# Later value products, quarter pieces as filler and more banks in the last attention stage of a one-core transformer kernel

## The reference, cut to what matters

```python
def _L1_xattn_ref(k, q, v):                      # k = v = context (16, 64, 512), q = layernorm(x)
    scores = jnp.einsum('bcn,bcm->bnm', k, q) / jnp.sqrt(jnp.float32(input_dim))
    attn = jax.nn.softmax(scores, axis=-1)       # over m: a 512 x 512 matrix for each batch entry
    return jnp.einsum('bnm,bcm->bcn', attn, v)
def _L1_ffn_ref(x, W_org, lora_down, lora_up, lora_keys, Wq):   # x = layernorm(x) of the new x
    base = jnp.einsum('bsi,oi->bso', x, W_org)
    q = jnp.einsum('bi,ki->bk', x.mean(axis=1), Wq)
    coeffs = jax.nn.softmax(jnp.einsum('bk,ek->be', q, lora_keys) / math.sqrt(K), axis=-1)
    h = jnp.einsum('bsi,eir->bser', x, lora_down)
    return base + jnp.einsum('be,bser,ero->bso', coeffs, h, lora_up)
x = x + _L1_xattn_ref(ctx, _layernorm(x), ctx)
x = x + _L1_ffn_ref(_layernorm(x), ...)
```

## Time and profile before

| | us |
|---|---|
| device time, median of 3 runs | 1195.75 (1193.85 to 1198.1) |
| device time of the profiled execution | 1194.14 |
| its span | 1192.3 |
| TensorE busy | 1124.5 (94%) |
| VectorE busy | 753.9 (63%) |
| ScalarE, GpSimd busy | 542.5 (46%), 416.8 (35%) |
| mean granted TensorE clock | 0.988 |

### The profile page before, as it was taken

How to read it: one execution, slowest core, us unless ns; L and a number is a source line. 1 busy time by engine, 2 the same in 40 slices (tenths; PEclk the granted TensorE clock), 3 DMA queues, 4 the chain that set the end, 5 groups by cost and what they waited for, 6 DMA issues and landing times. The chain is left out here.

```text
span 1192.3 us, 19230 instructions
## 1 busy us (share of the span) xinstructions
PE 1124.5 (94%) x6643; PEld 961.4 (81%) x6643; DVE 753.9 (63%) x1572; ACT 542.5 (46%) x1437; POOL 416.8 (35%) x421
## 2 busy tenths in 40 slices
PE   4899999999999999999999988799999999798998
PEld 3799999899899899999989887567777777676776
DVE  6555555555555555555555777889864666687863
ACT  4444454554544544544444545333323445454531
POOL 4443323323332232332332433144422324554531
PEclk9999999999999999999999999989999999898999
DMA  6211011111101101101100110122202245133300
GB/s 211 76 36 32 23 37 32 29 32 31 35 25 32 37 23 32 36 24 31 37 23 4 40 30 1 27 72 80 76 26 54 62 107 124 44 77 74 89 2 36
DMA packets 48716, 56.49 MB, mean 47 GB/s; under 512 B 10822, under 2 KB 29270, under 8 KB 48620
## 3 DMA queue, kind: packets, MB, share of 16 engines
q1 hardware_dynamic: 48620, 55.26, 17.2%
HBM read 40.56 MB, written 2.10 MB: 36 GB/s over the span
## 5 line engine op out<-in xcount | busy, mean ns | idle before, releaser
L378 PE MATMUL bank<-wqkv,kvT 128*128 128x256 f32 x1536 | 199.8, 286 | 8.7 <-DVE vv L566 8.7
L423 PE MATMUL bank<-wo,aoT 128*128 128x512 f32 x768 | 192.0, 399 | 5.7 <-DVE acc L562 5.7
L378 PEld LDWEIGHTS bank<-wqkv,kvT 128*128 128x128 f32 x1536 | 188.0, 192 | 10.4 <-DVE vv L566 10.4
L366 PE MATMUL bank<-wqkv,kvT 128*128 128x512 f32 x768 | 188.5, 395 | 1.7 <-DVE qn L576 1.7
L423 PEld LDWEIGHTS bank<-wo,aoT 128*128 128x128 f32 x768 | 139.5, 188 | 33.4 <-DVE aoT L557 6.3
L366 PEld LDWEIGHTS bank<-wqkv,kvT 128*128 128x128 f32 x768 | 141.5, 190 | 28.8 <-issue 1.8
L662 POOL TENSOR_TENSOR rms<-msq,half_neg 128x4 f32<-128x4 f32 x64 | 64.5, 1008 | 220.4 <-DVE msq L573 220.2
L874 PE MATMUL bank<-x2T,wgu 128*128 128x512 f32 (+1 forms) x336 | 91.5, 416 | 0.0
L549 ACT ACTIVATE prob<-bank,nmax 128x128 f32<-128x128 f32 x256 | 90.3, 372 | 2.1 <-DVE nmax L586 2.1
L1905 POOL TENSOR_TENSOR pr<-pr,rc 128x512 f32<-128x512 f32 x64 | 66.7, 1045 | 69.6 <-DVE rc L1774 69.5
L665 POOL TENSOR_TENSOR rms<-msq,half_neg 128x2 f32<-128x2 f32 x64 | 44.6, 697 | 132.0 <-DVE msq L582 132.0
(11 more groups left out here) (176 smaller groups left out, 2207.0 us busy)
## 6 DMA issues: line engine op xcount, KB each, us to landing
wqkv_raw<-in_L_xattn_Wq_dram SPq DMA_DIRECT2D x32, 256.0 KB, 2.5
wo_raw<-in_L_xattn_Wo_dram SPq DMA_DIRECT2D x32, 256.0 KB, 2.6
qS<-qhl SPq DMA_DIRECT2D x32, 256.0 KB, 3.7
kS<-chl SPq DMA_DIRECT2D x32, 128.0 KB, 3.0
packed<-_L_ffn_gate_qweight_dram SPq DMA_DIRECT2D x40, 64.0 KB, 2.4
packed<-in_L_ffn_up_qweight_dram SPq DMA_DIRECT2D x40, 64.0 KB, 2.3
packed<-_L_ffn_down_qweight_dram SPq DMA_DIRECT2D x10, 256.0 KB
acc<-in_x_dram SPq DMA_DIRECT2D x8, 256.0 KB, 5.7
```

The source lines that it names most:

```text
L366: mm = pe.matmul(b_q[:, :], kvT[:, l, kt, p, 1:3, :], wqkv[:, par, r, kt, 0:QW], start=(kt == 0 and n == 0), stop=(kt == KT - 1 and n == 2))
L378: mm = pe.matmul(b_kv[:, b * 256:(b + 1) * 256], kvT[:, l, kt, p, 2 * b:2 * b + 2, :], wqkv[:, par, r, kt, QW:QKV], start=(kt == 0 and n = ...
L423: mm = pe.matmul(b_o[:, :], aoT[:, l, h, :, :], wo[:, par, r, h, :], start=(h == 0 and n == 0), stop=(h == G - 1 and n == 2))
```

## The change

Up to tile 23 the lags stay at 5 and 6 steps. From tile 24 (FAR) on, the weights come 6 steps after the scores and the values 8 steps after, and the values are the last thing in TensorE's step. `pmT` and the row buffer `pr` get a third place each from FAR on. The scores have two banks (2 and 5) from tile 26, the weights two (3 and 7) from tile 22. `base` and `delta` are cut into quarters of 3 matmuls and placed by a new table; the first three quarters of a `base` already stand in steps 24 to 28. The small products get banks of their own and an own place (`pe_small`). The loop has 72 steps where it had 71.

```diff
-        LT, LV, LY = 5, 6, 10
-        SLOTS = TILES + LY - 3
+        SLOTS = TILES + 8
+        FAR = 6 * KT
+        TWO_S, TWO_T = 26, 22
...
+        def weights_slot(t):
+            return t + 5 if t < FAR else t + 6
+        def values_slot(t):
+            return t + 6 if t < FAR else t + 8
+        def sum_slot(n):
+            return values_slot(KT * n + KT - 1) + (n < FAR // KT)
...
-            return PT_ * (q - 1) + 6
+            return PT_ * q - 2 if PT_ * q <= FAR else PT_ * q + 5
...
-            return PT_ * p + 16
+            return sum_slot(2 * p + 1) + (2 if sum_slot(2 * p + 1) < WIDE else 3)
...
-            last = k >= WIDE or k == FFN_END
-            if last and 0 <= k - LV < TILES:
-                pe_values(pe, k - LV)
+            t = VALUES_AT.get(k)
+            last = t is not None and k == FFN_END
+            if last:
+                pe_values(pe, t)
             if k == FFN_END:
+                pe_late(pe, k, 0)
                 pe_extra(pe, k)
             pe_piece(pe, k, 0)
             if k != FFN_END:
                 pe_extra(pe, k)
+            pe_small(pe, k)
             pe_piece(pe, k, 1)
-            if not last and 0 <= k - LV < TILES:
-                pe_values(pe, k - LV)
+            if t is not None and not last:
+                pe_values(pe, t)
...
+        LATE = {
+            (24, 0): (("base", 0, 0),),
+            (25, 0): (("base", 0, 1),),
+            (28, 0): (("base", 0, 2),),
+            (30, 0): (("base", 0, 3),),
+            (32, 1): (("rank", 0, 0), ("rank", 0, 1),),
...
+            (47, 0): (("delta", 1, 3),),
+            (49, 0): (("base", 2, 0), ("base", 2, 1),),
+            (50, 1): (("rank", 4, 0), ("rank", 4, 1),),
...
         def pe_base(pe, p, r):
...
-                if p < HP and p % 2 == 0:
-                    pe.wait_ge(s_hv4, KT * (p // 2 + 1))
-                elif p < HP:
+                if p == 0:
+                    pe.wait_ge(s_hval, 2 * FT)
+                elif p <= HP:
                     pe.wait_ge(s_y4, p)
...
-            if r == 0:
-                pe.wait_ge(s_upl, KT)
-                pe.wait_ge(s_hl4, KT * (p // 2 + 1))
+            pe.wait_ge(s_hl4, KT * (p // 2) + r + 1)
...
-            if 25 <= k <= 28:
-                t = k - 25
+            if 30 <= k <= 33:
+                t = k - 30
                 act.wait_ge(s_ld_u, 16)
                 act.wait_ge(s_d, 2 * FT)
                 act.activation(up[:, HI, t, :], uraw[:, t, :], ACT.Copy).then_inc(s_uph, 1)
...
         def pe_l1f(pe):
+            for p in (4, 5):
+                for r in range(KT):
+                    pe_delta(pe, p, r)
+            pe_base(pe, 6, 0)
+            pe_base(pe, 6, 1)
             extra_evicted(pe, x4_slot(PAIRS - 2))
             x4_transposes(pe, PAIRS - 1)
```

More of the change, by code:

```diff
@@ L1243, in extra_evicted @@
                 pe.wait_ge(s_smc, 2)
-            elif kind == "query":
-                pe.wait_ge(s_smc, 3 + 2 * n)
-            elif kind == "scores":
-                pe.wait_ge(s_cv, 5 * n + 1)
-            else:
-                pe.wait_ge(s_smc, 4 + 2 * n)
+        SUMMED = {sum_slot(n): n for n in range(B)}
+        WEIGHTS_AT = {weights_slot(t): t for t in range(TILES)}
+        VALUES_AT = {values_slot(t): t for t in range(TILES)}
         def pair_at(k, first):
@@ L1449, in pe_values @@
                 pe.wait_ge(s_hval, FT + ALONE)
-            elif m == 0 and n == 6:
-                pe.wait_ge(s_y2, PAIRS)
+            elif n == FAR // KT - 1 and m == 0:
+                pe.wait_ge(s_y2, HP + 3)
             elif m == 0:
-                pe.wait_ge(s_ve, 2 * n if n < 6 else 2 * (n - 1))
+                pe.wait_ge(s_ve, 2 * n)
             pe.wait_ge(s_p1l, t + 1)
             for part in (HI, LO):
-                mm = pe.matmul(v_bank(n)[:, :], vS[:, q % 2, m, 2 * b:2 * b + 2, :], pmT[:, t % 2, part, :],
+                mm = pe.matmul(v_bank(n)[:, :], vS[:, q % 2, m, 2 * b:2 * b + 2, :], pmT[:, pm_of(t), part, :],
@@ L1468, in block_kernel @@
-        LATE.update({(61, 0): ("rank", 8), (62, 0): ("rank", 9), (63, 0): ("rank", 10), (64, 0): ("rank", 11),
-                     (64, 1): ("base", 4, 0), (65, 0): ("base", 4, 1), (65, 1): ("base", 5, 0),
-                     (66, 0): ("base", 5, 1), (66, 1): ("delta", 4, 0), (67, 0): ("delta", 4, 1),
-                     (69, 0): ("delta", 5, 0), (69, 1): ("delta", 5, 1), (70, 0): ("base", 6, 0)})
-        RANK_DONE = {k + 1: (piece[1],) for (k, h), piece in LATE.items() if piece[0] == "rank"}
@@ L1475, in pe_piece @@
+        RANK_DONE = {}
+        for (k, h), pieces in LATE.items():
+            for kind, n, r in pieces:
+                if kind == "rank" and r == 1:
+                    RANK_DONE.setdefault(k + 1, []).append(n)
+        DELTA_DONE = {k + 1: n for (k, h), pieces in LATE.items() for kind, n, r in pieces
+                      if kind == "delta" and r == KT - 1}
         def pe_piece(pe, k, h):
@@ new lines, in pe_base, with pe_rank @@
+            for k, (lp, rp) in enumerate(PASSES):
+                pe.matmul(m_o[p][:, :], x4_tile(lp, p)[:, r, :], woT[:, rp, r, :],
+                          start=(r == 0 and k == 0), stop=False)
+        def pe_rank(pe, n, r):
+            c, j = divmod(n, KT)
+            if r == 0:
+                pe.wait_ge(s_dnl, KT)
+                pe.wait_ge(s_x4l, 2 * (c + 1))
+                if j == 0 and c < 3:
+                    pe.wait_ge(s_smc, 4 + 2 * c)
+                elif n == 3 * KT + 1:
+                    pe.wait_ge(s_p1l, TILES)
+                elif n == 3 * KT + 2:
+                    pe.wait_ge(s_x4l, PAIRS)
+                    pe.wait_ge(s_mean, PAIRS)
+                elif n == 3 * KT + 3:
+                    pe.wait_ge(s_hv4, n - 2)
+                else:
+                    pe.wait_ge(s_hv4, n)
+            cols = slice(c % 2 * CW, (c % 2 + 1) * CW)
+            for kt in (2 * r, 2 * r + 1):
@@ L1595, in pe_extra @@
                 pe_key_scores(pe, n)
-            else:
+            elif kind == "weights":
                 pe_coefficients(pe, n)
@@ L1882, in dve_l1f @@
             x4_apply(dve, PAIRS - 1)
+            add_out(dve, 4)
             add_out(dve, 5)
@@ L1917, in pool_slot @@
                 pool_queries(pool, q + 1)
-            p = pair_at(k, PT_ + LY - KT)
-            if p is not None:
-                ln_power(pool, X4, p)
+            if k in SUMMED and SUMMED[k] % 2 == 1:
+                ln_power(pool, X4, SUMMED[k] // 2)
             if 20 <= k <= 23:
```

256 lines of the change are left out of this document (147 added, 109 removed).

## The result

| | median, us | runs |
|---|---|---|
| before | 1196.87 | 1193.85 to 1198.1, 4 runs |
| changed | 1184.45 | 1183.17 to 1185.31, 4 runs |

The ratio is 0.9899, with a 95% interval of 0.9876 to 0.9922: 9 to 15 us less. The forecast was 1177 (1168 to 1187).

A forecast was written before the change was run, and what follows sets the result against it. TensorE was taken to lose 36.1 us from step 24 on, largely waiting on a nearly equally loaded VectorE. Losses of 15.7 plus 2 for clock left 17.7, so 18.4 less; forecast median 1177 us, range 1168 to 1187.

The forecast's parts named there:

- queue rival: Waits at the head of VectorE's step tie TensorE through most of steps 31 to 63; 1182 to 1188 us, chance 0.27.
- hand walk: New lists walked step by step with measured durations; median 1177 us, own range 1170 to 1183, chance 0.62.
- The bare work: TensorE's work from step 24: 5.2, 10.4, 79.8 and 44.1 us by stretch, 139.5 against 139.4 before.
- Steps 25 to 30: VectorE has 14 to 15 us, TensorE 10.4; step 31 comes 14.9 us after step 25, lost 4.5.
- The clock: 2 us added for one or two clock drops, since a stall of 2 us still stands.
- Steps 31 to 63: TensorE has 79.8 us of work beside 80 of VectorE; 8.0 us lost.
- The waits at out(1) and at `rank`: Steps 31 to 51: 2.3 us for `base` of pair 2 behind out(1), and 0.4 to 1.1 at single `rank` products.
- Steps 64 on: Loss of 2.5 us: 0.8 for out(3), 0.6 for a `rank`, 1.1 at the last `x4` and the coefficients.
- I cost this at nothing: Steps 30 to 36: GpSimd gets about 17 us of work, covered by two steps; up to 2 us without cover.
- Values behind the pieces: Values two steps behind the weights, last in the step: the 2.10 us wait for the low part gets two steps of play.
- The clock rival: Low clock comes in steps 25 to 31 and stays or returns; at 60 us low the time is 1205, chance 0.05.
- The signs: Step 31 about 15 us after step 25, low-part waits nearly gone, VectorE about 90% busy, at most two low-clock stretches.

The follow-up runs named there:

- b_spread: Kernel before with the last three halves of `base` and `delta` of each couple moved by 1, 2 and 3 steps; 1193.12 us, ratio 0.9979.
- a_keys_first: Changed kernel with pair 4's normalised rows made early and the two stacked-key DMAs issued before the wait for the queries; 1183.94 us, ratio 0.9896.
- a_end: Changed kernel with pair 6's statistics in step 64, out(3) ahead of them, and pair 6's `x4` behind `rank` 8; 1181.36 us, ratio 0.9872.
- a_queries_early: Changed kernel with pair 4's normalised rows made ahead of entry 4's sum and copied ahead of the exponential; 1184.33 us, ratio 0.9894.

## Why the prediction was right, and where it was off

The side, the place and the kind of the gain were right, the size was too large: 18.8 us of gain were forecast against the median of its time, 12.4 came. The range held because it took in a part of the queue rival: the range that the hand walk gave itself, 1170 to 1183, doesn't hold 1184.45. In the profile the loss went from 36.1 to 24.6 us where 17.7 was forecast. The 6.9 us between them are 4.3 in steps 31 to 63 and 1.7 from step 64 on, both without the clock, 1.2 of clock, less 0.3 in steps 25 to 30. Less loss stands in step 24 (0.7 us), steps 25 to 30 (6.8) and steps 31 to 63 (6.1), more behind them (2.1): 11.5 gained. By its own steps:

- **The bare work** moved as counted (10.4, 79.8, 44.1), and **step 24** took 5.92 (forecast 5.9).
- **Steps 25 to 30**: forecast 14.9, measured 14.6. The second banks are 3.1 of it, shown by undoing them. The steps took 9.2 us less: 2.4 of less work and 6.8 of less loss, which I gave to this bank and to the query's own. I had left out the clock here. The 10.2 us at the low level before all lie in these steps, where I had priced them myself at 3.9, and none is there now. With the 3.1 that covers the 6.8, so the clock is a rival for what I gave to the query's bank. No run gives the query its old bank back, and whether that bank takes away the stall ahead of the drop stays open.
- **The clock**: two drops were allowed for with 2 us, two came and cost 3.2. Before, they cost 8. So nearly 5 of the 11.5 us gained is clock, 3.9 of it in steps 25 to 30. b_spread shows that part alone: a stall cut in two gives back the clock behind it and little else.
- **Steps 31 to 63**, the term that was too small: forecast a loss of 8.0, measured 93.6 - 79.8 = 13.8, or 12.3 without the clock, which had a term of its own. Of that 2.7 stand in step 31. The step that failed is "DMAs are the same and in the same order on SP's queue", priced at nothing. The queries of pair 4 had cover in the long steps 25 to 30, and those got 9 us shorter. The wait of a moved step for a DMA that didn't move was the first thing to look for. It would not have been enough to find it, as a_keys_first shows: the coefficients come as late.
- The waits at out(1) and at `rank` were forecast with 2.3 and 0.4 to 1.1, and the longest of each came with 0.9 and 1.0. By the starts of steps, 43 to 51 lost 4.2 in all, near the 4.7 forecast. Steps 36 to 42 lost 1.7, step 52 1.1 and steps 53 to 63 about 1, where I had none. The walk found the big stalls and missed most of the small ones, and its 8.0 should have carried a term for them.
- **Steps 64 on**: forecast a loss of 2.5, measured 53.2 - 3.2 - 44.1 = 5.9, 1.7 of it clock. "I cost this at nothing" was the step that failed for GpSimd: the cover of two steps is gone at the end, where the steps have no scores and hold as little as 1.2 us of TensorE's work (step 65). The reciprocal of tile 63 stands behind all of VectorE's step 63, and the weights wait 1.34, with a drop of the clock behind. a_end took 2.1 us of it back, beside the drop that didn't come.
- **Values behind the pieces**: I gave as reason the play between values and low part. The runs show another: the changed kernel has one value bank where it had two, and only with the values at the end is one enough. At the head it costs 6.8 us with a lag of 8, and 33 us with a lag of 6, with the clock in both. In the kernel before, which has two banks, moving the values to the end costs 4.7. No run has the new lags without the new table, or the quarters alone, so what each gives by itself in steps 31 to 63 stays open.
- **The rivals**: the time, 1184.45, lies in the one that I called tied to VectorE's queue (1182 to 1188), and its 13 us of loss in steps 31 to 63 are near the 13.8 measured. Its mechanism is borne out in part. Single waits taken away there (a_queries_early, a_keys_first) come back as others on the same queue. But the waits that it named, at `rank` and for out(p), make up only 3.5 us of the list of waits after. VectorE is busy 81.6 of 93.6 us there, 87%, where I had said about 90. The clock rival did not come: 6.8 us low, not 41.
- **The signs** that I had named came: step 31 starts 14.6 us after step 25, the profile names no wait of a value for the low part in steps 31 to 63, and VectorE's share is over 85%. Values and scores still wait 4.6 us there on TensorE's matmuls, close to the 5 that would have spoken against me, but for the DMA, for banks, and 1.5 of it where the profile names nothing.
- The page's rule on the ports shared by Vector and GpSimd (the Trainium skill, SBUF — State Buffer, Who interferes with whom) didn't bring the 2.7 us that I had put beside it: the normalised rows took 872 ns in the median, less than the 1284 before.

```profile
L1351 DVE TENSOR_SCALAR xn<-acc,mv,rs x4: 536/872/943, 1030.6 to 1094.9; 128x512 f32<-128x512 f32 x4
```

## What to carry to other kernels

When two engines carry nearly the same load, a wait in the profile names only the instruction that stands first, and not what is lost: before counting its time as a gain, ask what arrives second. If a stretch gets shorter, list everything that isn't moved and has to land in it, DMAs too. A change with several parts can hold one that pays for another (one bank less, and the place in the step that makes it bearable), so undo the parts one at a time before giving any of them the credit.
